# Output stage of a fused gate kernel: row scaling moved to ScalarE, the addition of x to GpSimd, one branch per group in place of four

## The reference

```python
xn = (x - mean(x)) / sqrt(var(x) + 1e-5)
s  = attn(xn)          # circular autocorrelation of the row; its 6 best lags; softmax of
                       # their values; the row rolled by each lag, summed with these weights
gate = silu(lin1(xn)); up = lin3(xn)      # 1024 -> 2752, weights tiled 4 times along the input
g  = silu(lin2(gate * up))                # 2752 -> 1024
out = x + s * g
```

## Time and profile before

| | |
|---|---|
| Median of 3 runs | 917.6 us (914.98 to 919.23) |
| The profiled execution | 914.26 us |
| Its span, first to last instruction | 912.4 us |
| Mean granted TensorE clock | 0.98 of full speed |
| TensorE busy | 845.7 us, 93% of the span |
| VectorE busy | 646.7 us, 71% |
| ScalarE busy | 307.5 us, 34% |
| GpSimd busy | 298.3 us, 33% |

### The profile page before, as it was taken

The page is one execution under the profiler, slowest core; times in us unless marked ns, Lnnn a source line. Parts: engine busy times, 40 slices in busy tenths (PEclk is TensorE's granted clock), DMA queues, the critical chain, the costliest instruction groups (busy, mean ns, idle before and its releaser), DMA issues.

```text
span 912.4 us, 11205 instructions
## 1 busy us (share of the span) xinstructions
PE 845.7 (93%) x4034; PEld 435.2 (48%) x4034; DVE 646.7 (71%) x1027; ACT 307.5 (34%) x456; POOL 298.3 (33%) x396
## 2 busy tenths in 40 slices
PE   3769777999999999999899999999999999999996
PEld 3323235634375335733375334843366343844365
DVE  7588986488956878387965979468965879443534
ACT  4654342233332333233232324233332333322231
POOL 5352540056403362055601373044600574000000
PEclk9889998999999999999999999999999999999998
DMA  9717020322223112321205012231114112130003
GB/s 310 230 29 244 29 52 1 118 93 64 53 71 140 36 29 52 117 93 35 70 24 198 15 50 53 93 117 35 44 38 163 48 41 29 48 139 1 1 1 140
DMA packets 53731, 71.70 MB, mean 79 GB/s; under 512 B 37146, under 2 KB 39418, under 8 KB 53380
## 3 DMA queue, kind: packets, MB, share of 16 engines
q1 hardware_dynamic: 53636, 70.67, 24.7%
HBM read 45.48 MB, written 16.78 MB: 68 GB/s over the span
## 4 chain that ended last, share of the span: by engine, by line
PE 57%; DVE 18%; DVEq 8%; issue 5%; POOL 5%; ACT 4%; DMA 3%; ACTq 0%; SPq 0%; POOLq 0%
PE g L1045 11%; PE u L1045 11%; PE g L1142 5%; PE u L1142 5%; DVEq L729 4%; PE u L1149 4%; PE u L1151 4%; PE g L1149 4%; PE g L1151 4%; PE zb L1121 4%; DVE h L713 3%; DVE junk L672 3%; DVE acc L725 2%; DMA ft<-ab 2%; DVEq L654 2%
## 5 line engine op out<-in xcount | busy, mean ns | idle before, releaser
L1045 PE MATMUL g<-xt,w_h 128*128 128x512 f16 x672 | 202.4, 383 | 12.6 <-DVE w_l L898 6.6
L1045 PE MATMUL u<-xt,w_h 128*128 128x512 f16 x672 | 202.4, 383 | 0.0
L501 ACT ACTIVATE sil<-g,winv 128x512 f32<-128x512 f32 (+1 forms) x176 | 118.9, 683 | 214.8 <-PE g L1062 154.3
L713 DVE SCALAR_TENSOR_TENSOR h<-u,winv,sil 128x512 f32<-128x512 f32 x168 | 124.5, 745 | 82.4 <-ACT sil L501 79.4
L672 DVE CUSTOM_DVE_ANT_0 junk<-xn,abc 128x1024 bf16<-128x1024 f32 x112 | 158.4, 1414 | 6.5 <-issue 2.2
L1045 PE MATMUL u<-xt,w_l 128*128 128x512 f16 x336 | 128.6, 383 | 0.0
L1045 PE MATMUL g<-xt,w_l 128*128 128x512 f16 x336 | 128.4, 382 | 0.0
L1045 PEld LDWEIGHTS u<-xt,w_h 128*128 128x128 f16 x672 | 66.3, 99 | 81.0 <-issue 2.8
L1045 PEld LDWEIGHTS g<-xt,w_h 128*128 128x128 f16 x672 | 57.0, 98 | 99.9 <-issue 41.7
L852 DVE SCALAR_TENSOR_TENSOR ob<-xr,c_mean,gg 128x1024 f32<-128x1024 f32 x32 | 41.1, 1285 | 82.3 <-ACT gg L501 80.9
L1142 PE MATMUL g<-w_h,hf_h 128*128 128x512 f32 x192 | 79.3, 413 | 14.0 <-DVE h L713 8.4
(11 more groups left out here) (164 smaller groups left out, 1212.9 us busy)
## 6 DMA issues: line engine op xcount, KB each, us to landing
xr<-in_x SPq DMA_DIRECT2D x34, 512.0 KB, 4.7
out_x<-ob SPq DMA_DIRECT2D x32, 512.0 KB, 2.9
xf<-in_x SPq DMA_DIRECT2D x30, 512.0 KB, 3.5
raw_w<-in_w2t SPq DMA_DIRECT2D x1, 2560.0 KB
raw_w<-in_w1t SPq DMA_DIRECT2D x3, 768.0 KB, 8.0
raw_w<-in_w3t SPq DMA_DIRECT2D x3, 768.0 KB, 9.8
abc<-in_a SPq DMA_DIRECT2D x1, 2048.0 KB, 13.6
xt<-hl SPq DMA_TRANSPOSE x32, 2.5
```

The costliest lines, as they stand in the source:

```text
L501: return nc.scalar.activation(out, in_, f, **kw)
L713: stt(out=h[0:n, p % NH, :], in0=up, scalar=winv[0:n, 2 * (p // 6) + 1:2 * (p // 6) + 2], in1=sil[0:n, p % 2, :], op0=ALU.mult, op1=ALU.mu ...
L1045: o = mm(bank[:], a, x, start=opens and t == 0, stop=closes and t == len(terms) - 1)
```

## The change

VectorE's second operation of a tile goes. ScalarE multiplies `gg` by rs, row by row, in a third instruction of 1024 columns. VectorE does ob = (x - mean) * gg alone. GpSimd adds x to ob, in place, behind its partition reduction of the same group. A new semaphore `scaled_done` tells VectorE that `gg` is scaled; `prod_done` tells ScalarE (the next tile's `gg`) and GpSimd that the product is there. `final_done`, for which the stores and the loads into `xr` wait, is now incremented by GpSimd. The branch is taken once a group: the four general bodies stand behind the If, the four short tiles behind the Else.

```diff
@@ gpsimd
                 nc.gpsimd.partition_all_reduce(rest_all[:], rest[:], P, RADD).then_inc(rall_done, 1)
+                for q in range(4):
+                    pool.wait_ge(prod_done, at_tile(i, q))
+                    tt(ob[q % 2][:], ob[q % 2][:], xrs[q % 2][:], ALU.add).then_inc(final_done, 1)
@@ scalar, tail_shifts(i)
-                    act.wait_ge(final_done, at_tile(i - 1, 3))
+                    act.wait_ge(prod_done, at_tile(i - 1, 3))
@@ scalar, down(i, q)
                 if i or q:
-                    act.wait_ge(final_done, at_tile(i, q - 1))
+                    act.wait_ge(prod_done, at_tile(i, q - 1))
                 for half, bank in enumerate((gb[DN[q]], ub[DN[q]])):
                     act.wait_ge(dn_ready, at_tile(i, q, 2, half + 1))
                     A(gg[:, 512 * half:512 * half + 512], bank[:], ACT.Silu).then_inc(dn_read, 1)
+                act.wait_ge(dn_read, at_tile(i, q, 2, 2))
+                A(gg[:], gg[:], scale=c_rs[:, q:q + 1]).then_inc(scaled_done, 1)
@@ vector, current(i)
-                    dve.wait_ge(final_done, at_tile(i - 1, 3))
+                    dve.wait_ge(prod_done, at_tile(i - 1, 3))
+                    dve.wait_ge(scaled_done, at_tile(i - 1, 3))
@@ vector, in place of final(i, q, flag)
-            def final(i, q, flag):
-                x, o = xrs[q % 2], ob[q % 2]
+            def tile_ready(i, q):
                 dve.wait_ge(xr_loaded[q % 2], 16 * (2 * i + q // 2 + 2))
-                dve.wait_ge(dn_read, at_tile(i, q, 2, 2))
+                dve.wait_ge(scaled_done, at_tile(i, q))
                 if i or q >= 2:
                     dve.wait_ge(stored[q % 2], 16 * (2 * i + q // 2))
-                stt(out=o[:], in0=x[:], scalar=c_mean[:, q:q + 1], in1=gg[:], op0=ALU.subtract, op1=ALU.mult)
-                drain()
-                with dve.If(flag > 0):
-                    correlate(q, x)
-                    exponentials()
-                    aggregate(o)
-                    tt(o[:], o[:], gg[:], ALU.mult)
-                    drain()
-                stt(out=o[:], in0=o[:], scalar=c_rs[:, q:q + 1], in1=x[:], op0=ALU.mult,
-                    op1=ALU.add).then_inc(final_done, 1)
+
+            def multiply(i, q):
+                tile_ready(i, q)
+                stt(out=ob[q % 2][:], in0=xrs[q % 2][:], scalar=c_mean[:, q:q + 1], in1=gg[:], op0=ALU.subtract,
+                    op1=ALU.mult).then_inc(prod_done, 1)
+
+            def general(i, q):
+                tile_ready(i, q)
+                correlate(q, xrs[q % 2])
+                exponentials()
+                aggregate(ob[q % 2])
+                tt(ob[q % 2][:], ob[q % 2][:], gg[:], ALU.mult).then_inc(prod_done, 1)
@@ vector, end of a group
-                for q in range(4):
-                    final(i, q, flag)
+                with dve.If(flag > 0):
+                    for q in range(4):
+                        general(i, q)
+                with dve.Else():
+                    for q in range(4):
+                        multiply(i, q)
```

More of the change, by code:

```diff
@@ L272, in build @@
         zh2_done, z2_read = sem("zh2_done"), sem("z2_read")
+        scaled_done, prod_done = sem("scaled_done"), sem("prod_done")
         dn_ready, dn_read, final_done = sem("dn_ready"), sem("dn_read"), sem("final_done")
```

## The result

The changed kernel takes 911.67 us (median of 4 runs, 911.45 to 912.35) where the kernel before takes 917.12 (4 runs, 914.98 to 919.23): ratio 0.9942, with 0.9918 to 0.9966 as its 95% interval. In the profiled executions the span went from 912.4 to 909.3 us, and the whole from 914.26 to 911.45; the prediction's own sum, made against that execution, was 914.7. The rest is that the forecast carried over 3.3 us by which the median of before stood above its profiled run (2.9 with the fourth run), where the median of after stands only 0.2 above its own.

A forecast was written before the change was run, and what follows sets the result against it. TensorE, busy 845.7 of 912.4 us, was taken to set the end. -2.37 (step-3 stalls) + 2.0 (end) + 0.8 (middle) = +0.4 on 914.26 gives 914.7; the median, 3.3 higher, gives 917.6 + 0.4 = 918.0, range 913.5 to 922.5.

The forecast's parts named there:

- step-3 gaps: TensorE's stalls at step 3 of groups 1, 3 and 5, waiting for VectorE's first product; all go: -2.37 us.
- long issue: 2.94 us in issue at the branch, between VectorE's two operations of the fourth tile; said to cause the step-3 stalls.
- GpSimd's addition: Adding x over 1024 columns on GpSimd: 2.4 us each, between 1.28 and 4.56; up to 4.75 costs the groups nothing.
- The tail: From the last gg to the last store, where nothing covers the longer chain: +2.0 us, bounds +0.9 and +4.2.
- The branch: One jump a group over four bodies, hidden while VectorE waits for the first scaled gg: zero cost.
- The loads of x: SyncE's queue: tile 2's load waits for GpSimd, may delay VectorE 1.1 us, covered by 4 us: cost zero.
- (b): Rival: the fourth GpSimd addition, stretched to 5.6 us, holds up the next group's spread: +6.4 us, 924; chance 0.10.
- (c): Rival: the middle stall becomes group 3's 1.05 us in all seven groups: +3.5 us, 921.1; chance 0.10.
- (d): Rival: the long issue is not the branch's and stays before the fourth product: +0.2 to +2.0 us, 919; chance 0.10.
- The middle of the groups: Step 9, transposing DMA to normalisation: groups 1 and 5 may become long like group 4; 0 to +1.6, taken +0.8 us.
- signs of being wrong: Additions over 4.75 us, a remaining gap at step 3, or middle gaps summing to under 2 or over 6 us.
- Rival (a): The middle stalls go too, because VectorE enters the step with less behind it: -3.8 us, 913.8; chance 0.12.

The follow-up runs named there:

- b_once: Kernel before with one If and Else around the four tiles instead of a branch in each, VectorE keeping both operations: 909.22 us, ratio 0.9923.
- b_far4: Kernel before with 128 never-run drains added in the general path of each group's fourth tile: 919.59 us, ratio 1.005.
- b_nobranch: Kernel before without the branch and the general path: 908.6 us, ratio 0.9917.
- a_pad64: Changed kernel with 64 never-run drains in group 0's general path, so VectorE's later code lies 64 rows further: 910.51 us, ratio 0.9942.
- a_copy: Changed kernel with c_rs and c_mean doubled and their copies made ahead of the flag's use: 911.25 us, ratio 0.9957.

## Why the prediction was wrong

**Right, by its steps.** The step-3 gaps are those of the long issue in the fourth tile: b_once takes only that away and they go, b_far4 puts it into every group and they come. GpSimd's addition: 2.4 forecast, 2.39 measured. VectorE starts 2.35 to 2.4 behind gg, forecast 2.52. The tail: +2.0 forecast, +1.7 measured, of which the branch gives 0.5 and the arithmetic costs 2.2. The branch hides in the wait for the first tile (b_nobranch). The loads of x cost nothing with a single branch: the page of after puts all of VectorE's idle time before the product, 155.6 us, down to gg. Rivals (b), (c) and (d) did not come.

**The step that failed: "The middle of the groups".** It stood at 0 to +1.6, taken as +0.8. Measured: of the four gaps, 3.44 us, one of 1.05 is left, and groups 2, 4 and 6 are 1.1 to 1.2 us shorter each, as the table has it. The prediction said that the DMA takes 3.59 or 2.48 "for a reason that the trace doesn't show". The trace had it beside the late landing: the same window's DMA view has the instruction packet, and the page has 64 of them on q14. The prediction did not read that view. With it the step reads: the change takes VectorE's instruction packets from 64 to 41, since it no longer jumps out of what it holds once or twice a group; the late landings of groups 2, 4 and 6 have VectorE's packet, group 3's has TensorE's own; three go, one stays. That is -2.4 us by the gaps and -3.4 by the periods, in place of +0.8. With the other two terms (-2.37 + 2.0) on 914.26 it makes 911.5 and 910.5 for an execution that measured 911.45. Two of the prediction's own signs of being wrong came: middle gaps of under 2 us in sum, and a gap at step 3 that remains. How many late landings fall away is partly luck of where the code lies. In a_pad64 one of VectorE's packets meets the third transposing DMA of group 3 and makes it 1.0 us late, where nothing waits for it.

**Rival (a)** had the sign and nearly the size, but with a wrong mechanism: VectorE's earlier start. b_once keeps VectorE's work and has the whole gain.

**A term that was missed, and its rule applied too narrowly.** The first product was to come 5.5 us behind gg with 2.1 to spare. It comes at 7.55, the spare time is 0.1 or less, and in group 1, where 0.27 us of issue stand before it as well, it is short by 0.36. What used up the spare time is the copy of c_rs, 2.37 us in all seven ends of groups. The Trainium skill ("SBUF — State Buffer", section on the two separate sides) puts under the lock both VectorE operations with two SBUF inputs and those in a two-port performance mode. The prediction asked only for the former and passed the statistics; the copies, which stand directly behind the product, it did not list. The trace agrees with the lock, with 2.35 of addition and 2.37 of copy that end together, and a_copy with 0.17; which mode the copy runs in, no trace says.

**The last part is measurement.** The forecast carried over the 3.3 us between the profiled run of before and its median. After's runs lie within 0.9 us of each other, so nothing of that kind was there to carry. Between profiled executions such differences lie mostly ahead of the end of group 0, which is spread over 3.7 us among the kernels here; what makes them is open.

## What to carry to other kernels

A branch is paid not only in the engine that jumps: ask the DMA view of each late transfer whether an instruction packet ran in its window, and try the branch alone before the arithmetic around it. When work is moved to GpSimd, list every VectorE instruction that can start beside it, the four-column copies too, and ask whether there is slack to pay for it. And where TensorE sets the end and the last tile has no cover, a longer chain of engines per tile is a loss at the tail, however idle the engines are.

## What the runs showed of the hardware

- VectorE's jump over 128 drains more leaves 2.8 to 3.1 us of idle issue in every group (b_far4). A jump that doesn't miss leaves some 0.6 us between the two operations (before), where b_once, without a jump there, has 0.07. The Trainium skill ("Runtime: NRT & Kernel Launch", section on instruction fetch mechanics) has a taken branch to a target outside the current two pages force a DMA of the target page before execution goes on; the traces agree in kind, and the price here is 2.8 to 3.2 us in before.
- Instruction packets of 8 KB (VectorE, mostly 0.3 to 0.6 us) or 16 KB (TensorE, about 1.0 us) that begin 1.8 to 2.1 us behind the issue of the transposing DMA lengthen its landing from 2.55 us to 3.4 to 4.25 for the first such DMA of a group, and to 3.1 or more for the other three. One that began 0.5 us behind it gave 3.37, one 0.24 us ahead of it gave 2.54. A data packet of 0.47 us and 5.5 KB at the same moment gave 2.8. Why the one costs more than the other stays open.
- A late landing of 1.7 us costs its group 1.7 us (105.11 against 103.36 in b_once), though TensorE's gap in it is only 1.04. The next wait in the group is 0.17 longer (1.32 against 1.15), two more of 0.09 and 0.13 stand around the gap, and the last 0.3 is longer busy time of TensorE, by the windows of groups 2 and 3 of b_once:
```profile
280.32:383.68 103.36, 102.21 (x499) 52.70 (x499) 78.21 (x123) 34.08 (x52) 38.37 (x49) 1.00 0.23 72
383.68:488.79 105.11, 102.53 (x499) 52.54 (x499) 78.10 (x123) 33.69 (x51) 37.85 (x49) 1.00 0.23 71
```
  The first two numbers of a row are the stretch and TensorE's busy time, in us.
- A copy of four float32 columns on VectorE takes 2.37 us when a GpSimd addition of 2.35 began 0.01 us before it, and 0.17 without one (a_copy).
